# Earlier gathers, other places for the raw weights, split weights in halves and attention adds in three groups, in a one-core attention and mixture-of-experts kernel

## The reference

```python
x = L0_attn_x                       # (2, 1024, 256) float32, 2048 tokens
xn = layernorm(x)
# attention, 16 heads of 16, without a softmax over keys
q = elu(heads(xn @ Wqk + bqk)); k = q
v = heads(silu(xn @ Wv + bv)); u = silu(xn @ Wu + bu)
kv = einsum('bhnd,bhne->bhde', k, v)
a = u * layernorm(merge(einsum('bhnd,bhde->bhne', q, kv)), ln_g, ln_b)
attn = a @ Wo + bo
# experts: 8 of them, the 2 best for each token, hidden width 512
probs = softmax(xn @ gate_w.T); w, idx = top_k(probs, 2); w = w / w.sum()
expert_e(t) = (silu(t @ w1[e].T) * (t @ w3[e].T)) @ w2[e].T
ffn = sum over the token's 2 experts of w * expert(xn)
out = x + attn + ffn
```

## Time and profile before

| | |
|---|---|
| median of 3 runs | 304.72 us (304.63 to 308.46) |
| the profiled execution | 301.63 us |
| its span | 299.9 us |
| PE busy | 242.4 us, 81% |
| DVE busy | 189.9 us, 63% |
| ACT busy | 152.0 us, 51% |
| POOL busy | 135.3 us, 45% |
| mean granted clock of TensorE | 0.95 of full speed |

### The profile page before, as it was taken

How to read it: one execution, slowest core, us unless ns; L and a number is a source line. 1 busy time by engine, 2 the same in 40 slices (tenths; PEclk the granted TensorE clock), 3 DMA queues, 4 the chain that set the end, 5 groups by cost and what they waited for, 6 DMA issues and landing times.

```text
span 299.9 us, 6061 instructions
## 1 busy us (share of the span) xinstructions
PE 242.4 (81%) x1784; PEld 158.6 (53%) x1784; DVE 189.9 (63%) x413; ACT 152.0 (51%) x255; POOL 135.3 (45%) x128
## 2 busy tenths in 40 slices
PE   0327998996678886999999999999999979989400
PEld 0117776874455443576666666666566545555200
DVE  3998799499874798685859586867674323333000
ACT  2876784186568661736374545455564323434100
POOL 6375000173300005667874672747265564316561
PEclk9999799999977997999999999999999999999765
DMA  6999992088935339999999999899989999797552
GB/s 209 412 420 407 424 427 107 0 212 237 183 59 76 59 78 119 139 177 146 170 170 130 153 210 127 119 138 178 181 107 152 147 172 124 132 150 109 82 58 32
DMA packets 86290, 50.48 MB, mean 168 GB/s; under 512 B 72547, under 2 KB 83811, under 8 KB 85061
## 3 DMA queue, kind: packets, MB, share of 16 engines
q1 hardware_dynamic: 76516, 35.42, 52.7%
q0 software_dynamic: 9744, 14.69, 32.1%
HBM read 23.35 MB, written 11.67 MB: 117 GB/s over the span
## 4 chain that ended last, share of the span: by engine, by line
PE 29%; DMA 13%; DVE 9%; issue 8%; POOLq 6%; ACT 5%; POOL 1%; ACTq 0%; DVEq 0%
PE bank L1144 16%; PE bank L1157 8%; DMA out<-regions,row_out 5%; POOLq L452 5%; DMA out<-xn 4%; DVE regions L748 3%; ACT regions L527 3%; PE bank L1196 3%; DMA xrow<-xrow 2%; DMA out<-area,row_out 2%; DVE xrow L940 2%; PE bank L1173 1%; PE bank L1185 1%; POOL out L461 1%; DVE xrow L945 1%
## 5 line engine op out<-in xcount | busy, mean ns | idle before, releaser
L1144 PE MATMUL bank<-regions,xg_all 128*128 x468 | 108.9, 384 | 3.9 <-DMA xg_all<-regions 2.1
L1144 PEld LDWEIGHTS bank<-regions,xg_all 128*128 128x128 f16 x468 | 44.6, 99 | 54.7 <-issue 8.2
L1157 PE MATMUL bank<-regions,xrow 128*128 x468 | 59.7, 280 | 7.5 <-DMA xrow<-xrow 7.4
L1157 PEld LDWEIGHTS bank<-regions,xrow 128*128 128x128 f16 x468 | 46.1, 100 | 21.7 <-issue 10.6
L613 ACT ACTIVATE xrow<-xrow 128x512 f16<-128x512 f32 x39 | 24.6, 630 | 58.5 <-DVE xrow L940 58.5
L940 DVE SCALAR_TENSOR_TENSOR xrow<-bank,xrow 128x512 f32<-128x512 f32 x39 | 26.9, 691 | 38.4 <-PE bank L1144 35.2
L461 POOL DMA_INDIRECT out<-area,row_out x20 | 33.6, 1680 | 30.9 <-issue 13.3
L461 POOL DMA_INDIRECT out<-regions,row_out x19 | 31.2, 1643 | 28.7 <-issue 17.5
L439 POOL DMA_INDIRECT xrow<-xsplit,row_in x8 | 11.3, 1408 | 66.4 <-DMA xg_all<-xrow 33.4
L945 DVE TENSOR_TENSOR xrow<-xrow 128x512 f16<-128x512 f32 x39 | 26.9, 690 | 21.6 <-ACT xrow L613 21.6
L608 ACT ACTIVATE xrow<-bank 128x512 f32<-128x512 f32 x39 | 23.2, 595 | 27.7 <-PE bank L1144 27.5
(11 more groups left out here) (150 smaller groups left out, 304.1 us busy)
## 6 DMA issues: line engine op xcount, KB each, us to landing
regions<-wexp SPq DMA_DIRECT2D x8, 1536.0 KB, 13.9
xsplit<-xrow SPq DMA_DIRECT2D x4, 512.0 KB, 9.6
out<-xn POOLq DMA_DIRECT2D x8, 256.0 KB
area<-x SPq DMA_DIRECT2D x2, 768.0 KB, 7.7
regions<-wattn SPq DMA_DIRECT2D x1, 1032.0 KB, 10.6
xrow<-xrow SPq DMA_TRANSPOSE x39
area<-x SPq DMA_DIRECT2D x1, 512.0 KB, 3.5
regions<-xsplit,row_in POOLq DMA_INDIRECT x31, 4.7
```

Source lines behind the costliest of these rows:

```text
L1144: last = mm(bank_[:], xg[t % 4][:, KD * d + k, :], w16[:, bass.ds(e, 1), w, at:at + I].rearrange("p a c -> p (a c)"), start=(k == 0 and n ...
L1157: last = mm(ps_y[t % 2][:, 0:D], hT[t % 2][:, IC * d + c, :], w16[:, bass.ds(e, 1), w, at:at + D].rearrange("p a c -> p (a c)"), start=(c ...
```

## The change

1. The raw weights move. Experts 0 and 1 are loaded into regions 8 and 9 instead of 2 and 3, experts 2 to 6 into e + 1 instead of e + 2, and expert 7 into region 8, when expert 0's are split. `hi(2)`, `hi(3)` and `hi(4)` wait for `w_lo` 2, 3 and 4 instead of 1, 2 and 3. SP's order of loads changes with it: expert 1 is loaded after the attention weights are split, ahead of the last of four stores of the split tokens.
2. Region 9 is free once expert 1 is split. Twelve tiles (4 to 15) are gathered into it in the front. Tiles 16 to 19 are gathered in the loop ahead of the adds of tiles 8 to 11, the others with the groups.
3. Experts 5 to 7 are split in halves of 1536 columns: the first on each engine at the end of the front, then one in each of iterations 0 to 4, on ACT behind `h_hi(t)`, on DVE at the end of the iteration.
4. The attention pairs are added in groups of three, three and two, ahead of the adds of tiles 13, 22 and 28. Each group first issues two gathers, then waits for the adds, issues its pairs, the other gathers (six, six, one), and waits for the pairs.

```diff
@@ -65,10 +65,14 @@
 EARLY = 5
+HALF = WCOLS // 2
+RAW = (E, E + 1) + tuple(range(3, E)) + (E,)
 FEW = 4
-PLACES = 16
+MANY = 12
+MORE = 8
+PLACES = FEW + MANY + MORE
 PAIR_AT = [4 + 3 * p for p in range(NP)]
-FIN_AFTER = {PAIR_AT[2 * i + 1] + 4: (2 * i, 2 * i + 2) for i in range(NP // 2)}
+GROUPS = {PAIR_AT[2] + 3: (0, 3, 20, 28), PAIR_AT[5] + 3: (3, 6, 28, 36), PAIR_AT[7] + 3: (6, 8, 36, ST)}
 ROUTE_WORDS = 3 * TT * E + 2 * TOPK * TT * E + 6 * TT + TOPK * TT + E * TT + 3 * E + E * E \
@@ -179,7 +183,8 @@
         xgr = [view(stage, I * 6 + D * r, [2 * D], F16) for r in range(FEW)]
-        xgr += [view(regions, E * WCOLS + D * (4 + r), [2 * D], F16) for r in range(PLACES)]
+        xgr += [view(regions, (E + 1) * WCOLS + D * r, [2 * D], F16) for r in range(MANY)]
+        xgr += [view(regions, E * WCOLS + D * (4 + r), [2 * D], F16) for r in range(MORE)]
         h16 = [view(stage, I * (2 + r), [2, I], F16) for r in range(2)]
@@ -301,11 +308,11 @@
-            return t % FEW if t < 2 * FEW else FEW + t % PLACES
-
-        def visit(t):
-
-            return t // FEW if t < 2 * FEW else (t - 2 * FEW) // PLACES
+            return t if t < PLACES else FEW + t - PLACES
+
+        def raw(e):
+
+            return regions[:, RAW[e] * WCOLS:(RAW[e] + 1) * WCOLS]
@@ -324,7 +331,7 @@
             def load_expert(e):
-                sp.dma_start(regions[:, (e + 2) * WCOLS:(e + 3) * WCOLS], wexp[e]).then_inc(raw_loaded[e], 16)
+                sp.dma_start(raw(e), wexp[e]).then_inc(raw_loaded[e], 16)
             def store_split(c):
@@ -332,13 +339,19 @@
             load_expert(0)
+            load_expert(2)
+            store_split(0)
+            load_expert(3)
+            store_split(1)
+            load_expert(4)
+            store_split(2)
+            sp.wait_ge(attn_lo, 1 + KD)
             load_expert(1)
-            for c in range(TT // CH):
-                store_split(c)
-                load_expert(2 + c)
-            load_expert(E - 2)
-            sp.wait_ge(attn_lo, 1 + KD)
-            load_expert(E - 1)
+            store_split(3)
+            load_expert(5)
+            load_expert(6)
+            sp.wait_ge(w_lo, 1)
+            load_expert(7)
@@ -346,7 +359,7 @@
             def load_x(t):
-                sp.wait_ge(gathered[place(t)], 16 * (visit(t) + 1))
+                sp.wait_ge(gathered[place(t)], 16 * (1 + t // PLACES))
                 wait(sp, b_done, t - 3)
@@ -430,12 +443,13 @@
             def gather(t):
-                if FEW <= t < 2 * FEW:
-                    pool.wait_ge(xg_loaded[t % 4], 16)
-                if t == 2 * FEW:
-                    pool.wait_ge(w_lo, E)
-                if t >= 2 * FEW + PLACES:
-                    pool.wait_ge(xg_loaded[t % 4], 16 * ((t - PLACES) // 4 + 1))
+                if t == FEW:
+                    pool.wait_ge(w_lo, 2)
+                if t == FEW + MANY:
+                    pool.wait_ge(late_lo, 2 * (E - EARLY))
+                if t >= PLACES:
+                    done = t - PLACES + FEW
+                    pool.wait_ge(xg_loaded[done % 4], 16 * (done // 4 + 1))
                 g.indirect_dma_start(xgr[place(t)], None, xsplit,
@@ -444,7 +458,7 @@
             g.dma_start(out[TOKENS:TOKENS + SPARE, :], x[0:SPARE, :]).then_inc(y_added[1], 16)
-            for t in range(FEW, 2 * FEW):
+            for t in range(FEW, FEW + MANY):
                 gather(t)
@@ -461,25 +475,26 @@
-            def add_attention(p0, p1, n):
-
+            def add_attention(n, p0, p1, t0, t1):
+
+                for t in range(t0, t0 + 2):
+                    gather(t)
                 for i in range(2):
...
                                 accum_op=ALU.add).then_inc(fin_added, 16)
-                for t in range(2 * FEW + PLACES + 3 * p0, min(ST, 2 * FEW + PLACES + 3 * p1)):
+                for t in range(t0 + 2, t1):
                     gather(t)
...
             for t in range(ST):
-                if t in FIN_AFTER:
-                    add_attention(*FIN_AFTER[t], t)
-                for later in range(2 * FEW + 2 * (t - 2), 2 * FEW + 2 * (t - 1)):
-                    if 2 * FEW <= later < 2 * FEW + PLACES:
-                        gather(later)
+                if t in GROUPS:
+                    add_attention(t, *GROUPS[t])
+                if 8 <= t < 12:
+                    gather(t + 8)
                 add_expert(t)
@@ -519,12 +534,18 @@
-            def raw(e):
-                return regions[:, (e + 2) * WCOLS:(e + 3) * WCOLS]
-
             def hi(e):
...
                 a.activation(w16[:, e, 0, :], raw(e), ACT.Copy, scale=SCALE).then_inc(w_hi, 1)
+
+            def hi_half(n):
+                e, part = EARLY + n // 2, slice(HALF * (n % 2), HALF * (n % 2 + 1))
+                if n == 0:
+                    act.wait_ge(w_lo, EARLY)
+                elif n % 2 == 0:
+                    act.wait_ge(late_lo, n)
+                act.wait_ge(raw_loaded[e], 16)
+                a.activation(w16[:, e, 0, part], raw(e)[:, part], ACT.Copy, scale=SCALE).then_inc(late_hi, 1)
@@ -580,24 +601,25 @@
             halves(1)
-            act.wait_ge(w_lo, 1)
+            act.wait_ge(w_lo, 2)
             hi(2)
...
             halves(2)
-            act.wait_ge(w_lo, 2)
+            act.wait_ge(w_lo, 3)
             hi(3)
...
             halves(4)
-            act.wait_ge(w_lo, 3)
+            act.wait_ge(w_lo, 4)
             hi(4)
...
             halves(7)
+            hi_half(0)
             a.activation(warm[:], log_scale[:], ACT.Silu).then_inc(warm_done, 1)
@@ -619,7 +641,7 @@
                 if t == 4:
-                    act.wait_ge(w_lo, 7)
+                    act.wait_ge(late_lo, 2 * (E - EARLY))
                 if t >= RING:
@@ -651,9 +673,6 @@
             for t in range(ST + 2):
-                if t < E - EARLY:
-                    act.wait_ge(w_lo, EARLY - 1 + t)
-                    hi(EARLY + t)
                 if phase(t, 2) is not None:
@@ -664,6 +683,8 @@
                     h_hi(t)
+                if t + 1 < 2 * (E - EARLY):
+                    hi_half(t + 1)
                 if phase(t, 0) is not None:
@@ -745,8 +766,14 @@
                 dve.wait_ge(w_hi, e + 1)
-                v.scalar_tensor_tensor(w16[:, e, 1, :], regions[:, (e + 2) * WCOLS:(e + 3) * WCOLS], SCALE,
+                v.scalar_tensor_tensor(w16[:, e, 1, :], raw(e), SCALE,
                                        w16[:, e, 0, :], ALU.mult, ALU.subtract).then_inc(w_lo, 1)
+
+            def expert_lo_half(n):
+                e, part = EARLY + n // 2, slice(HALF * (n % 2), HALF * (n % 2 + 1))
+                dve.wait_ge(late_hi, n + 1)
+                v.scalar_tensor_tensor(w16[:, e, 1, part], raw(e)[:, part], SCALE,
+                                       w16[:, e, 0, part], ALU.mult, ALU.subtract).then_inc(late_lo, 1)
@@ -931,6 +958,7 @@
             kv_lo(1)
+            expert_lo_half(0)
@@ -1003,8 +1031,8 @@
                     finish(phase(t, 3))
-                if t < E - EARLY:
-                    expert_lo(EARLY + t)
+                if t + 1 < 2 * (E - EARLY):
+                    expert_lo_half(t + 1)
@@ -1132,8 +1160,10 @@
-                if t < E:
+                if t < EARLY:
                     pe.wait_ge(w_lo, t + 1)
+                elif t < E:
+                    pe.wait_ge(late_lo, 2 * (t + 1 - EARLY))
                 e = expert_of(t)
```

More of the change, by code:

```diff
@@ L216, in build @@
         w_lo = sem("w_lo")
+        late_hi = sem("late_hi")
+        late_lo = sem("late_lo")
         shift_ready = sem("shift_ready")
@@ L245, in build @@
         tiles_ready = sem("tiles_ready")
-        gathered = [sem(f"gathered{r}") for r in range(FEW + PLACES)]
+        gathered = [sem(f"gathered{r}") for r in range(PLACES)]
         k_done = sem("k_done")
```

## The result

The changed kernel takes 314.52 us, the median of four runs (311.40 to 315.21), against 304.68 us for the kernel before, in four runs beside them. The ratio is 1.0335, with a 95% interval from 1.0225 to 1.0444: slower by 3.3%. The prediction of 305.4 us and its range up to 310.5 were wrong. The profiled execution took 314.4 us for a span of 312.6, so 12.7 us more span than before. I split this by five marks: the start of tile 0 on PE, of tile 4's second product and of the last product, the end of tile 38's output on ACT, and the start of the last add on POOL.

The account below looks back on a forecast made before the run. Taken as bounds: the front, the expert tiles on PE, and POOL's late adds. Span 299.9 + 8.5 - 0.7 - 6.1 - 1.0 = 300.6 us, so 305.4 us as measured; range 300.5 to 310.5 (0.78).

Parts of the forecast that it names:

- The waits at the front, +7.1: Front: ACT's splits wait for later DVE splits and hold what stands behind, so the front ends 7.1 us late.
- Rival 1: Front: the waits' delay never reaches PE, so 7.1 us go and the time is 298.2 us; 8 in 100.
- The load of expert 1, +1.4: Front: expert 1's load, issued later, lands late and delays ACT's hi(1) by 1.4 us.
- PE already waited 0.49 us: Front, at 39.62: PE already waited for outputs behind hi(1), so nothing absorbs the late load, taken as +1.4 us.
- a clock loss at the loop's start: First tiles: PE's products run partly at the lower clock after waiting some 5 us; 0 to 2 us, taken as 0.9.
- The first tiles, -0.7: Tile 0 to tile 4's second product: half splits win a net 0.7 us (bounds -1.6 and +0.4).
- POOL's backlog, -6.1: End of the kernel: fewer loop gathers and drains let POOL's last add start on time, winning 6.1 us.
- The whole -6.1 is won: End: POOL is early by some 3 us at tile 38, so its entire 6.1 us backlog goes and PE is last.
- PE's stops in the loop, -1.0: Tile loop: fewer gathers but pairs by three shrink PE's waits for transposes by 1.0 us (bounds -3.6 and +1).
- rival 2: Tile loop: bursts of three pairs delay transposes and stop PE, +6 to +9 us net, 312 to 315 us; 10 in 100.
- The front as a whole: Up to tile 0 on PE: waits and late load together +8.5 us, bounds +7.1 and +9.1.

Follow-up runs that it names:

- change_again: The changed kernel once more, unchanged, for a second profile; ratio 1.0313 against the kernel before.
- halves_only: The kernel before with only experts 5 to 7 split in halves, at the change's points; ratio 1.0036 against the kernel before.
- groups_only: The kernel before with only its attention pairs in three groups, ahead of the adds of tiles 13, 22 and 28; ratio 0.9980 against the kernel before.
- four_groups: The changed kernel with the pairs in four groups of two, ahead of tiles 11, 17, 23 and 29; ratio 1.0198 against the kernel before.
- groups_at_starts: The kernel before with its four groups of two pairs moved ahead of adds 13, 18, 23 and 28; ratio 0.9896 against the kernel before.
- gathers_in_loop: The changed kernel with tiles 8 to 15 gathered in the loop, two ahead of each of adds 2 to 5; ratio 1.0411 against the kernel before.

## Why the prediction was wrong, step by step

- **The waits at the front, +7.1: right.** Both stops stand in the profile with their lengths (7.21 and 4.03 us), and the price from `hi(1)` to tile 0 is 7.5 us. Rival 1 (8 in 100) is refuted: ACT held all that stood behind the wait.
- **The load of expert 1, +1.4: right for the load, but the clock behind it was left out.** ACT waited 1.36 us for the load. But the whole term came to 3.8 us in the first profile: `hi(1)` was 2.1 us late, 0.7 of this from earlier steps, and I took "PE already waited 0.49 us" as the end of it. The longer stop, 1.96 us, was followed by U projections 1.7 us longer at the lower clock. I had counted a clock loss at the loop's start and none here. change_again, with a stop of 2.06 us, had none either, so this part comes in some executions only.
- **The first tiles, -0.7: wrong in sign, small.** It was +0.7, and +1.5 in change_again. The halves won what I had forecast: tile 3's h_mul stands 17.0 us behind tile 0's start on PE instead of 20.2. Nearly all of it went at the first attention step, whose turn on PE comes only 0.7 us earlier by that count. Behind it stood the clock, for which 0.9 us was too little: in that row alone it was 4.12 - 2.75 = 1.4, and 1.7 in halves_only. The kernel before had lost as much to the clock two tiles earlier (2.56 and 3.39 us at 116.37 and 118.72), so PE's busy time in the stretch is no longer than before (27.9 us against 28.1); its idle time is, 5.9 against 5.0.
- **POOL's backlog, -6.1: right in kind, too large.** It was -4.3 (add 38 is 3.7 us behind its output, not 1.9). "The whole -6.1 is won" gave POOL 3 us of slack that it didn't have; only without pair adds is it 2.1 behind.
- **PE's stops in the loop, -1.0: the step that failed most.** It was +6.2 in the first profile and +2.8 in change_again (156.75 against 153.91). Where I had PE's stops shrink, they grew. I had set fewer gathers against larger bursts and let the gathers decide. The row for it was there, the 2.13 us stop behind a group, but I took the two groups of before behind which PE didn't stop as proof for groups of other size, at other tiles. groups_only shows +3.5 us from the new groups alone, and without pair adds PE's idle time falls to 4.9 us. This is close to rival 2's mechanism, which I had at +6 to +9 and 10 in 100; at about a third to a half of its price it was the likelier reading. The first profile's extra 3.4 us are 2.6 of lower clock, some of it behind such a stop, and 0.7 more of idle time.
- **The sum.** Forecast +8.5 - 0.7 - 6.1 - 1.0 = +0.7 us of span; measured in the first profile +11.3 + 0.7 - 4.3 + 6.2 - 1.3 = +12.6, in the second +9.7 + 1.5 + 2.8 - 4.9 and no change at the last product, so +9.1. The front as a whole (+9.1 at most) and the stops in the loop (+1 at most) both came out above their upper bounds, in both profiles, so the range, made from them, ended too low.
- **Still open:** how much of the 2.8 us in the loop is the size of the bursts, how much their places and the gathers beside them, and how much chance (1.6 us of it stand ahead of the last product, 32 us behind the last group; four_groups differs from the change by less than its interval), and what groups_at_starts wins by.

## What to carry to other kernels

A buffer freed earlier is paid for by whoever must wait for it: before moving a buffer, look whether what it makes room for is worth anything (here not: with eight of the twelve early gathers put back, gathers_in_loop takes as long as the change). When bulk transfers are grouped anew, book a stop of the latency-bound transfers beside them (in groups_only 3 us of PE's time) against the synchronisation saved. And where PE already waits a little, a longer wait can cost more than itself, since the products behind it may run at the lower clock (here 1.7 us behind a stop of 1.96, in one of two profiles).

## What was unexpected of the hardware

The indirect gathers of POOL in the front take 0.95 us to issue, but 2.96 and 3.59 when they start inside one of DVE's 3.35 us splits. The one that started 0.16 us ahead of a split took 1.06. POOL's and DVE's timelines of the change:

```profile
77.91 1.06 POOL L453 DMA_INDIRECT regions<-xsplit,row_in  x1 [0.30 <-issue]
79.28 2.96 POOL L453 DMA_INDIRECT regions<-xsplit,row_in  x1 [0.30 <-issue]
...
87.54 3.59 POOL L453 DMA_INDIRECT regions<-xsplit,row_in  x1 [0.30 <-issue]
```
```profile
78.07 3.35 DVE L769 SCALAR_TENSOR_TENSOR regions<-regions 128x3072 f16<-128x3072 f32 x1
...
86.96 3.35 DVE L769 SCALAR_TENSOR_TENSOR regions<-regions 128x3072 f16<-128x3072 f32 x1
```

Both end 0.82 us after the split beside them (82.24 and 81.42, 91.13 and 90.31), so I read it as a wait for its end, not a slower rate. The Trainium skill, page "SBUF — State Buffer", section "SBUF: two separate sides", describes the pair of ports that VectorE and GpSimd share as a lock that whichever starts first holds for its whole instruction. By the same section a VectorE operation with two SBUF inputs takes it too, but only against a GpSimd operation that reads SBUF. This split has two such inputs, the gather reads its row numbers (`row_in`) from SBUF, and the trace agrees. The last gather ended at 92.4 and its first user is past 110, so it cost nothing here.

The clock's share was larger than I had thought: stops of only 2 to 3 us are followed by 12 products at 3.84 to 4.48 us instead of 2.76. Not every such stop has this behind it: the change's two profiles differ by 1.6 us at tile 0, all of it clock, and by 3.4 us in the loop, 2.6 of it clock.
